# State attention of a fused transformer kernel: value products before state products, and both halves of four groups of work in a row between projections

## The chip, the cores and the metric

The kernel runs on one NeuronCore of a Trainium2 chip. A core has TensorE (PE in the profile; its weight loads are PEld), VectorE (DVE), ScalarE (ACT), GpSimd (POOL) and SyncE (SP), which issues the DMAs. Each engine works through its own list of instructions in order, and they meet at semaphores. The metric is the device time of one execution in microseconds; less is better.

## The reference

Four layers over 1024 tokens of 256 features, each an attention and a feed-forward part, run as one program. The change lies in the attention of layer 2, which goes through 64 slots per head:

```python
q = (hs @ Wq.T).reshape(B, T, H, DK)      # T = 1024 tokens in the kernel, H = 16, DK = DV = 128
k = (hs @ Wk.T).reshape(B, T, H, DK)      # both are rotated (rope)
v = (hs @ Wv.T).reshape(B, T, H, DV)
s = clip(hs @ Ws1.T @ Ws2.T + bs2)        # M = 64 slots per head
es = jnp.exp(s)
enz = jnp.exp(-cumlogsumexp(s))
A = where(mask, einsum('bhtd,bhjd->bhtj', q, k) * scale, 0.0)
ok = enz * jnp.einsum('bhtj,bhjm->bhtm', A, es)
qv = jax.nn.softmax(ok, axis=-1)
W2 = where(mask, einsum('bhtm,bhjm->bhtj', qv * enz, es), 0.0)
o = jnp.einsum('bhtj,bhjd->bhtd', W2, v)
o_n = o * rsqrt(mean(o * o) + EPS) * g_norm_weight
return (o_n * silu(g)).reshape(B, T, H * DV) @ Wo.T
```

## The kernel before

`state_attention` takes the 16 heads in eight pairs (`PAIRS`); the two heads of a pair are `a_` = 0 and 1. The 1024 tokens are eight blocks of 128 (`t`), four of them a half (`h` = 0 or 1, 512 tokens). The masked product over all earlier tokens is split: inside a block it is done with the 128x128 scores or weights (`atw`), and what lies before the block comes from a running state of 64 slots per head (`s1` for keys, `s2` for values), in which head 0 has partitions 0 to 63 and head 1 has 64 to 127.

One step `p` of the loop over pairs holds the work of pair `p`, the projections of pair `p + 1` and the last part of pair `p - 1`. TensorE's order is written out by hand in `_(pe)`, and so are those of ScalarE, VectorE and GpSimd. The groups of TensorE that matter here:

- `project(p + 1, c, h)` (q and k of the next pair): six fp32r matmuls of 128x512 (`gemm3`, line 718), and `out_product(p - 1, h, m)`, six alike.
- `turn_sums(p, h)` and `turn_soft(p, h)`: four transposes of 128x128 each (line 2437), of the sums over slots and of the softmax.
- `weights(p, h)`: W2 of a half, eight fp32 matmuls with 64 rows each, the two heads in the upper and the lower half of the array (`tile_position`, line 2532).
- `outputs(p, h)`: per block two value products with all 128 rows (`atw` by `v`, line 2549) and then two state products with 64 rows (`pb` by `s2`, line 2552), block by block; both add into the PSUM bank of the head. Block `t` = 0 has no state products.
- `key_states(p, h)` early in the step (line 2475): keys by exponentials of the slots.

Each PSUM bank (128x512) has a list of uses (`step_uses`), by which `opens` waits until the use before it has been emptied.

Who follows TensorE: `shift` (VectorE, maximum and difference behind `turn_sums`), `exp_soft` (ScalarE), `divide` (VectorE behind `turn_soft`), `copy_weights` (ScalarE, line 2664) and `mask_weights` (GpSimd, line 2853) behind `weights`; `outputs(p, h)` waits for the masks. Behind outputs come `square` (ScalarE, line 2748), `gate` (VectorE, line 3034) and `sum_squares` (3042). Behind each projection come `swap` (ScalarE, lines 2737 and 2738), `sines` (GpSimd, line 2873), `cosines` (VectorE, 3016) and `rotate` (VectorE, 3025). On VectorE the end of a step is gates of half 1, sums, rotations, and `clip` of the next pair's slot scores; then ScalarE takes their exponential (`exp_slots`, line 2672), then `root`, values and gates, and the key copies (`copy_keys`, line 2648) for which `key_states` waits.

Of the kernel before, what the change touches and what calls it, by code (L numbers as in the profile page):

```python
# [33 lines left out]
def half(h):  # L34
    return slice(h * HALF, (h + 1) * HALF)
# [2189 lines left out]
def state_attention(nc, core, a):  # L2225
# [18 lines left out]
        + [(("vg", 2, j), 0, 4 + j) for j in range(2)] + [(("ok", 0), 0, 0)]  # L2244
        + [(("to", 1, a_), -1, 2 + a_) for a_ in range(2)] + [(("ok", 1), 0, 1)]
        + [(("vg", 3, j), 0, 6 + j) for j in range(2)] + [(("s2", h), 0, 4 + h) for h in range(NH)]
# [3 lines left out]
        + [(("w2", 0, a_), 0, 2 + a_) for a_ in range(2)] + [(("q", 1, 1), 1, 7)]  # L2250
        + [(("w2", 1, a_), 0, a_) for a_ in range(2)] + [(("q", 2, 0), 1, 4)]
        + [(("o", 0, a_), 0, 2 + a_) for a_ in range(2)] + [(("q", 2, 1), 1, 5)]
        + [(("o", 1, a_), 0, a_) for a_ in range(2)] + [(("q", 3, 0), 1, 6), (("q", 3, 1), 1, 7)])
    uses = [(("ls", h), -1, h) for h in range(NH)]
    uses += [(k, s + dp, b) for s in range(-1, len(PAIRS)) for k, dp, b in step_uses if s + dp in PAIRS]
    uses += [(("to", 0, a_), LAST, 4 + a_) for a_ in range(2)] + [(("wo", 0, 0), LAST, 6), (("to", 1, 0), LAST, 2)]
# [15 lines left out]
    with ExitStack() as ctx:  # L2272
# [33 lines left out]
        v = sb("v", [P, TB, 2, DK])  # L2306
# [6 lines left out]
        atw = sb("atw", [P, TB, 2, P])  # L2313
# [18 lines left out]
        def bank(key):  # L2332
            return core.bank[bank_of[key]]
# [4 lines left out]
        def wait_emptied(eng, key):  # L2338
            b, n = emptying[key]
            eng.wait_ge(emptied[b], n)  # L2340
# [4 lines left out]
        def opens(pe, key):  # L2345
            if before[key] is not None:
                wait_emptied(pe, before[key])
# [41 lines left out]
        def _(pe):  # L2389
# [21 lines left out]
            def project(p, c, h):  # L2411
                if p not in PAIRS:
                    return
                key = ("q", p, c, h)
                pe.wait_ge(qkw_split, 2 * (4 * p + c) + 2)
                opens(pe, key)
                gemm3(pe, bank(key)[:, :], [qkwh[:, c, k * P:(k + 1) * P] for k in range(DC)],
                      [qkwl[:, c, k * P:(k + 1) * P] for k in range(DC)],
                      [core.xh[:, k, half(h)] for k in range(DC)],
                      [core.xl[:, k, half(h)] for k in range(DC)]).then_inc(full[bank_of[key]], 1)  # L2420
# [75 lines left out]
            def turn_sums(p, h):  # L2496
                if p not in PAIRS:
                    return
                wait_emptied(pe, ("ok", p, h))
                turn(("tok", p, h), lambda b: oke[:, (4 * h + b) * P:(4 * h + b + 1) * P])  # L2500
# [14 lines left out]
            def turn_soft(p, h):  # L2515
                if p not in PAIRS:
                    return
                pe.wait_ge(soft_exped, 2 * p + h + 1)
                turn(("tq", p, h), lambda b: qv[:, (4 * h + b) * P:(4 * h + b + 1) * P])
# [17 lines left out]
            def outputs(p, h):  # L2537
                if p not in PAIRS:
                    return
                keys = [("o", p, h, a_) for a_ in range(2)]  # L2540
                pe.wait_ge(w2_ready, 4 * p + 2 * h + 2)
                wait_emptied(pe, ("s2", p, h))
                opens(pe, keys[0])
                opens(pe, keys[1])
                for b in range(4):
                    t = 4 * h + b
                    for a_ in range(2):
                        out = bank(keys[a_])[:, b * P:(b + 1) * P]
                        mm = pe.matmul(out, atw[:, t, a_, :], v[:, t, a_, :], start=True, stop=t == 0)
                    for a_ in range(2 if t else 0):  # L2550
                        r = slice(64 * a_, 64 * a_ + 64)
                        mm = pe.matmul(bank(keys[a_])[:, b * P:(b + 1) * P], pb[r, t * P:(t + 1) * P], s2[r, t, :],
                                       start=False, stop=True, tile_position=(64 * a_, 0))
                        if b == 3:
                            mm.then_inc(full[bank_of[keys[a_]]], 1)

# [6 lines left out]
            def out_product(p, h, m):  # L2563
                if p not in PAIRS:
                    return
                key = ("wo", p, h, m)
                pe.wait_ge(wo_split, 2 * p + 2)
                wait_emptied(pe, ("to", p, h, 0))
                wait_emptied(pe, ("to", p, h, 1))
                opens(pe, key)  # L2570
                gemm3(pe, bank(key)[:, :], [woh[:, a_, m * P:(m + 1) * P] for a_ in range(2)],
                      [wol[:, a_, m * P:(m + 1) * P] for a_ in range(2)], [ogh[:, a_, half(h)] for a_ in range(2)],
                      [ogl[:, a_, half(h)] for a_ in range(2)]).then_inc(full[bank_of[key]], 1)
# [3 lines left out]
            for p in range(-1, len(PAIRS)):  # L2577
                turn_slots(p, 0)
                turn_slots(p, 1)
                turn_keys(p, 0, 0)  # L2580
                turn_keys(p, 0, 1)
                scores(p, 0, 0)
                scores(p, 0, 1)
                slot_scores(p + 1)
                values(p, 0)
                turn_keys(p, 1, 0)
                turn_keys(p, 1, 1)
                scores(p, 1, 0)
                scores(p, 1, 1)
                values(p, 1)  # L2590
                key_states(p, 0)
                key_states(p, 1)
                turn_out(p - 1, 0, 0)
                turn_out(p - 1, 0, 1)
                values(p, 2)
                slot_sums(p, 0)
                turn_out(p - 1, 1, 0)
                turn_out(p - 1, 1, 1)
                slot_sums(p, 1)
                values(p, 3)  # L2600
                value_states(p, 0)
                value_states(p, 1)
                out_product(p - 1, 0, 0)
                turn_sums(p, 0)
                out_product(p - 1, 0, 1)
                turn_sums(p, 1)
                out_product(p - 1, 1, 0)
                out_product(p - 1, 1, 1)
                project(p + 1, 0, 0)
                turn_soft(p, 0)  # L2610
                project(p + 1, 0, 1)
                turn_soft(p, 1)
                project(p + 1, 1, 0)
                weights(p, 0)
                project(p + 1, 1, 1)
                weights(p, 1)
                project(p + 1, 2, 0)
                outputs(p, 0)
                project(p + 1, 2, 1)
                outputs(p, 1)  # L2620
                project(p + 1, 3, 0)
                project(p + 1, 3, 1)
# [926 lines left out]
```

## Time and profile before

| | |
|---|---|
| median of 3 runs | 2773.91 us (2773.88 to 2775.19) |
| the profiled execution | 2764.51 us, its span 2762.8 us |
| TensorE busy | 2515.4 us, 91% of the span |
| VectorE, GpSimd, ScalarE busy | 1625.1, 1290.9, 1259.8 us |
| state attention | from about 1787 to 2286 us of the span |

How to read it: busy time is the sum of an engine's instructions. Records of TensorE's matmuls overlap (one of 0.40 us starts 0.23 us after the last), so in a list of its instructions the distance from start to start says what they cost. PEclk is the share of full clock granted to TensorE. In a timeline the columns are start, duration, engine, line, operation, what it writes and reads, count, and in brackets the idle time before it with what ended it.

### The profile page before, as it was taken

The page shows a single profiled execution, that of the slowest core. Times are in us where ns is not written, and L with a number is a line of the kernel's source. Part 1 is how long each engine was busy: PE and PEld are TensorE (multiplying, and loading weights), DVE is VectorE, ACT ScalarE, POOL GpSimd, SP SyncE. Part 2 cuts the span into 40 slices and gives each one's busy share as a digit, 9 for nine tenths or more (in the row PEclk, how much of TensorE's full clock was granted, in tenths as well). Part 3 has the DMA queues.
Part 4 walks back from the last instruction along what each step waited for, and adds up shares of the span by engine and source line. Part 5 has one row for each costly group of instructions (what it writes and reads, how often), then busy time and mean ns, then how long its engine had stood idle before and what let it go on. Part 6 is the DMA issues. An engine that isn't in the chain of part 4 may idle for free. (4 is left out here: it accounts for less than half of the span.)

```text
span 2762.8 us, 40694 instructions
## 1 busy us (share of the span) xinstructions
PE 2515.4 (91%) x14474; PEld 1675.7 (61%) x14474; DVE 1625.1 (59%) x2163; ACT 1259.8 (46%) x2174; POOL 1290.9 (47%) x1130
## 2 busy tenths in 40 slices
PE   6887999888999999999878878889999988998798
PEld 4443777654444444444564436678888877776676
DVE  4663555576766766665336543477777745555655
ACT  4464333464555555555434652256655643333322
POOL 4100344486888888888630002255454533442243
PEclk9798999998999999999976989899999999999899
DMA  1000111121101111010000001100010001110111
GB/s 59 1 2 11 39 46 46 48 80 39 39 16 39 31 31 39 16 35 1 25 26 1 1 1 49 47 20 28 20 32 20 20 5 42 46 46 21 31 41 43
DMA packets 39710, 81.63 MB, mean 30 GB/s; under 512 B 7553, under 2 KB 21121, under 8 KB 39041
## 3 DMA queue, kind: packets, MB, share of 16 engines
q1 hardware_dynamic: 39264, 79.41, 10.2%
q8 instruction: 98, 1.61, 0.2%
q14 instruction: 60, 0.48, 0.1%
q10 hardware_dynamic: 288, 0.13, 0.0%
HBM read 59.07 MB, written 2.62 MB: 22 GB/s over the span
## 5 line engine op out<-in xcount | busy, mean ns | idle before, releaser
L2019 DVE TENSOR_REDUCE a1h_mseg<-bank 128x2 f32<-128x1024 f32 x256 | 302.6, 1221 | 187.2 <-PE bank L1776 173.2
L63 POOL TENSOR_TENSOR f_wh<-f_raw,ones_r 128x768 fp32r<-128x768 f32 (+1 forms) x74 | 112.5, 1520 | 534.9 <-PE bank L462 360.0
L1953 ACT ACTIVATE a1h_prob<-bank 128x512 f32<-128x512 f32 x366 | 206.1, 598 | 165.6 <-PE bank L1836 83.8
L1756 POOL TENSOR_TENSOR a_qk<-a_qk,a1h_prob 128x512 f32<-128x512 f32 x186 | 238.9, 1318 | 50.8 <-ACT a1h_prob L1953 50.8
L451 PE MATMUL bank<-x_norm_h,f_wh 128*128 128x512 f32 x592 | 243.1, 411 | 6.7 <-PEq L3249 2.5
L451 PE MATMUL bank<-x_norm_l,f_wh 128*128 128x512 f32 x592 | 237.5, 401 | 0.0
L451 PE MATMUL bank<-x_norm_h,f_wl 128*128 128x512 f32 x592 | 237.0, 400 | 0.0
L658 DVE SCALAR_TENSOR_TENSOR f_tf<-bank,f_bias,f_sg 128x512 f32<-128x512 f32 x148 | 110.9, 750 | 187.2 <-PE bank L451 180.8
L542 ACT ACTIVATE f_hhi<-f_hf 128x512 fp32r<-128x512 f32 x124 | 78.3, 632 | 275.6 <-DVE f_hf L666 275.6
L1834 PE MATMUL bank<-a1h_ql,a1h_k 128*128 128x512 f32 x512 | 203.2, 397 | 0.0
L1849 PE MATMUL bank<-a1h_prob,a_v 128*64 128x512 f32 x732 | 179.9, 604 | 0.0
L672 DVE TENSOR_TENSOR f_hlo<-f_hf,f_hhi 128x512 fp32r<-128x512 f32 x124 | 116.2, 939 | 82.7 <-ACT f_hhi L542 82.4
L531 ACT ACTIVATE f_sg<-bank,f_bias 128x512 f32<-128x512 f32 x148 | 102.0, 689 | 128.4 <-PE bank L451 128.3
L451 PEld LDWEIGHTS bank<-x_norm_h,f_wh 128*128 128x128 f32 x592 | 113.5, 192 | 50.8 <-issue 24.3
L362 POOL TENSOR_TENSOR f_wl<-f_raw,f_wh 128x768 fp32r<-128x768 f32 (+1 forms) x74 | 128.0, 1730 | 5.9
L451 PEld LDWEIGHTS bank<-x_norm_l,f_wh 128*128 128x128 f32 x592 | 113.7, 192 | 28.1
L451 PEld LDWEIGHTS bank<-x_norm_h,f_wl 128*128 128x128 f32 x592 | 113.8, 192 | 24.9
L462 PE MATMUL bank<-f_hhi,f_wh 128*128 128x512 f32 x296 | 118.4, 400 | 10.4 <-DVE f_hlo L672 10.4
L1833 PE MATMUL bank<-x_norm_h,a1h_kn 128*128 128x512 f32 x256 | 120.4, 470 | 4.5 <-DVE a1h_k L2014 3.3
L2873 POOL TENSOR_TENSOR l2a_rope<-l2a_rope,l2a_tab 128x512 f32<-128x512 f32 x64 | 81.4, 1279 | 88.7 <-ACT l2a_rope L2738 87.7
L1756 POOL TENSOR_TENSOR x_norm<-x_norm,a1h_prob 128x512 f32<-128x512 f32 x86 | 112.4, 1340 | 20.5 <-ACT a1h_prob L1953 20.5
L1833 PE MATMUL bank<-x_norm_l,a1h_kn 128*128 128x512 f32 x256 | 118.6, 463 | 0.9
(597 smaller groups left out, 6277.1 us busy)
## 6 DMA issues: line engine op xcount, KB each, us to landing
f_raw<-in_l_w_dram SPq DMA_DIRECT2D x66, 385.0 KB, 3.0
a1h_st_q<-a_qk SPq DMA_DIRECT2D x128, 128.0 KB, 2.4
l2a_qkraw<-in_l2a_wqk_dram SPq DMA_DIRECT2D x32, 128.0 KB, 2.1
l2a_vraw<-in_l2a_wvg_dram SPq DMA_DIRECT2D x8, 512.0 KB, 3.7
f_raw<-in_l_w_dram SPq DMA_DIRECT2D x8, 449.0 KB, 3.3
a_qk<-l_keys SPq DMA_DIRECT2D x24, 128.0 KB, 2.7
a1p_raw<-in_l1a_w_dram SPq DMA_DIRECT2D x20, 128.0 KB, 2.1
a_qk<-in_l1a_wo_dram SPq DMA_DIRECT2D x16, 128.0 KB, 2.1
```

The source lines that it names most:

```text
L63: return pool.tensor_tensor(dst, src, one.to_broadcast(list(src.shape)), ALU.mult)
L362: pool.tensor_tensor(wl[:, slot, :], raw[:, slot, 0:B], wh[:, slot, :].bitcast(F32), ALU.subtract).then_inc(w_split, 1)
L451: mm = pe.matmul(out[:, :], w[:, slot, c0:c0 + P], x, start=n == 0, stop=n == 3 * n_k - 1)
L462: mm = pe.matmul(acc[m][h][:, :], w[:, slot, c0:c0 + P], x[:, h, :], start=begin and n == 0, stop=False, skip_group_check=True)
L658: dve.scalar_tensor_tensor(tf[:, h, :], up[h][:, :], bias[:, slot, 1:2], sg[:, h, :], ALU.add, ALU.mult).then_inc(t_ready, 1)
L672: dve.tensor_tensor(hl[:, h, :], src[:, h, :], hh[:, h, :].bitcast(F32), ALU.subtract).then_inc(hl_ready, 1)
L1756: pool.tensor_tensor(out, first, slot_of[t % NP], ALU.add).then_inc(sum_done, 1)
L1833: pe.matmul(bank[:, :], kn[:, G % 2, a, keys], QA[n % 2][:, a, half(h)], start=True, stop=False)
L1834: mm = pe.matmul(bank[:, :], k1[:, a, keys], ql[:, n % 2, a, half(h)], start=False, stop=lo >= hi)
L1849: pe.matmul(core.bank[5][64 * a:64 * a + 64, :], v[:, kb, 2 * (n // 4) + a, :], slot_of[t % NP], start=kb == 0, stop=kb == TB - 1, skip_gr ...
L1953: act.activation(slot_of[t % NP], core.bank[2 + t % 3][:, :], ACT.Exp, scale=scale).then_inc(p_ready, 1)
L2019: dve.tensor_reduce(mseg[:, :, qb, s], spare(("A", n, k))[:, :, :], AX.X, ALU.max).then_inc(a_read, 1)
```

## The change

Three things, all in `state_attention`. In `outputs` all value products of a half come first and its state products then, each half with one run of either (the `start` flag is now set for the first block of a bank alone). In TensorE's order both halves of `turn_sums`, of `turn_soft`, of `weights` and of `outputs` stand behind one another, between two projections or products, where a projection stood between the halves before. `step_uses` follows that order. The lists of the other engines are unchanged.

```diff
@@ step_uses
-        + [(("wo", 0, 0), -1, 0), (("tok", 0), 0, 2), (("wo", 0, 1), -1, 1), (("tok", 1), 0, 3)]
+        + [(("wo", 0, 0), -1, 0), (("wo", 0, 1), -1, 1), (("tok", 0), 0, 2), (("tok", 1), 0, 3)]
...
@@ outputs
                     for a_ in range(2):
                         out = bank(keys[a_])[:, b * P:(b + 1) * P]
-                        mm = pe.matmul(out, atw[:, t, a_, :], v[:, t, a_, :], start=True, stop=t == 0)
+                        mm = pe.matmul(out, atw[:, t, a_, :], v[:, t, a_, :], start=b == 0, stop=False,
+                                       skip_group_check=True)
+                for b in range(4):
+                    t = 4 * h + b
                     for a_ in range(2 if t else 0):
                         r = slice(64 * a_, 64 * a_ + 64)
                         mm = pe.matmul(bank(keys[a_])[:, b * P:(b + 1) * P], pb[r, t * P:(t + 1) * P], s2[r, t, :],
-                                       start=False, stop=True, tile_position=(64 * a_, 0))
+                                       start=False, stop=b == 3, tile_position=(64 * a_, 0), skip_group_check=True)
@@ the order of TensorE in a step
                 out_product(p - 1, 0, 0)
+                out_product(p - 1, 0, 1)
                 turn_sums(p, 0)
-                out_product(p - 1, 0, 1)
                 turn_sums(p, 1)
                 out_product(p - 1, 1, 0)
                 out_product(p - 1, 1, 1)
                 project(p + 1, 0, 0)
+                project(p + 1, 0, 1)
                 turn_soft(p, 0)
-                project(p + 1, 0, 1)
                 turn_soft(p, 1)
                 project(p + 1, 1, 0)
+                project(p + 1, 1, 1)
                 weights(p, 0)
-                project(p + 1, 1, 1)
                 weights(p, 1)
                 project(p + 1, 2, 0)
+                project(p + 1, 2, 1)
                 outputs(p, 0)
-                project(p + 1, 2, 1)
                 outputs(p, 1)
                 project(p + 1, 3, 0)
                 project(p + 1, 3, 1)
```

TensorE's list at the outputs of a pair before the change (value products are line 2549, state products 2552, a projection's matmuls line 718), from the first block on:

```order
L2549 MATMUL bank<-l2a_v,l2a_atw 128x128 x4
L2552 MATMUL bank<-l2a_s_,l2a_pb_ 128x128 x2
L2549 MATMUL bank<-l2a_v,l2a_atw 128x128 x2
L2552 MATMUL bank<-l2a_s_,l2a_pb_ 128x128 x2
L2549 MATMUL bank<-l2a_v,l2a_atw 128x128 x2
L2552 MATMUL bank<-l2a_s_,l2a_pb_ 128x128 x2
L718 MATMUL bank<-x_norm_h,l2a_qkwh 128x512
...
L2549 MATMUL bank<-l2a_v,l2a_atw 128x128 x2
L2552 MATMUL bank<-l2a_s_,l2a_pb_ 128x128 x2
```

The same place after the change (the lines have moved to 2550 and 2556):

```order
L718 MATMUL bank<-x_norm_l,l2a_qkwh 128x512
L2550 MATMUL bank<-l2a_v,l2a_atw 128x128 x8
L2556 MATMUL bank<-l2a_s_,l2a_pb_ 128x128 x6
L2550 MATMUL bank<-l2a_v,l2a_atw 128x128 x8
L2556 MATMUL bank<-l2a_s_,l2a_pb_ 128x128 x8
L718 MATMUL bank<-x_norm_h,l2a_qkwh 128x512
```

Seven runs of state products have become two, and the projection between the halves has moved ahead of both. At the weights (line 2532) TensorE's list before the change reads:

```order
L2532 MATMUL bank<-l2a_pb_,l2a_es_ 128x128 x8
L718 MATMUL bank<-x_norm_h,l2a_qkwh 128x512
L718 MATMUL bank<-x_norm_h,l2a_qkwl 128x512
L718 MATMUL bank<-x_norm_l,l2a_qkwh 128x512
L718 MATMUL bank<-x_norm_h,l2a_qkwh 128x512
L718 MATMUL bank<-x_norm_h,l2a_qkwl 128x512
L718 MATMUL bank<-x_norm_l,l2a_qkwh 128x512
L2532 MATMUL bank<-l2a_pb_,l2a_es_ 128x128 x8
```

And after the change (there it is line 2533), with the end of the projection that now stands ahead of them:

```order
L718 MATMUL bank<-x_norm_h,l2a_qkwh 128x512
L718 MATMUL bank<-x_norm_h,l2a_qkwl 128x512
L718 MATMUL bank<-x_norm_l,l2a_qkwh 128x512
L2533 MATMUL bank<-l2a_pb_,l2a_es_ 128x128 x16
L718 MATMUL bank<-x_norm_h,l2a_qkwh 128x512
```

Two runs of eight have become one of sixteen; the turns (line 2437) go from four and four to eight in the same way.

## Rows read from the trace of the kernel before

**Rows 1.** Stretches: busy us of PE, PEld, DVE, ACT, POOL, PEclk, DMA, GB/s; one step.

```profile
1957.00:2015.50 58.50, 58.03 (x422) 48.04 (x418) 42.10 (x64) 34.53 (x57) 29.06 (x31) 1.00 0.08 23
```

**Rows 2.** Timeline of TensorE, weights and outputs of one step.

```profile
1968.81 1.16 PE L2532 MATMUL bank<-l2a_pb_,l2a_es_ 64*128 64x128 f32 x16
1969.90 0.51 PE L718 MATMUL bank<-x_norm_h,l2a_qkwh 128*128 128x512 f32 x1
...
1973.87 0.39 PE L718 MATMUL bank<-x_norm_l,l2a_qkwh 128*128 128x512 f32 x1
1974.10 1.05 PE L2549 MATMUL bank<-l2a_v,l2a_atw 128*128 128x128 f32 x8
1975.08 0.49 PE L2552 MATMUL bank<-l2a_s_,l2a_pb_ 64*128 64x128 f32 x4
1975.50 0.71 PE L2549 MATMUL bank<-l2a_v,l2a_atw 128*128 128x128 f32 x4
1976.14 0.49 PE L2552 MATMUL bank<-l2a_s_,l2a_pb_ 64*128 64x128 f32 x4
...
1977.63 0.50 PE L718 MATMUL bank<-x_norm_h,l2a_qkwh 128*128 128x512 f32 x1
...
1979.13 0.61 PE L2549 MATMUL bank<-l2a_v,l2a_atw 128*128 128x128 f32 x4
1979.67 0.49 PE L2552 MATMUL bank<-l2a_s_,l2a_pb_ 64*128 64x128 f32 x4
...
1983.28 0.51 PE L718 MATMUL bank<-x_norm_h,l2a_qkwh 128*128 128x512 f32 x1
```

**Rows 3.** Timeline of TensorE, turns of four and of eight.

```profile
1966.89 0.60 PE L2437 MATMUL bank<-ident,x_norm 128*128 128x128 f32 x4
1967.24 0.48 PE L718 MATMUL bank<-x_norm_h,l2a_qkwh 128*128 128x512 f32 x1
1967.56 0.40 PE L718 MATMUL bank<-x_norm_h,l2a_qkwl 128*128 128x512 f32 x1
...
1986.18 1.03 PE L2437 MATMUL bank<-ident,l2a_es_ 128*128 128x128 f32 x8
```

**Rows 4.** Timeline of TensorE, before the key states of the next pair.

```profile
1998.73 0.40 PE L718 MATMUL bank<-l2a_vgl,x_norm_h 128*128 128x512 f32 x1
1999.34 3.31 PE L2475 MATMUL bank<-l2a_estm,l2a_ktm 128*128 128x64 f32 x28 [0.21 <-ACT l2a_ktm L2648]
```

**Rows 5.** Timeline of VectorE, gates of half 0 to gates of half 1.

```profile
1978.36 1.29 DVE L3034 TENSOR_TENSOR l2a_og<-bank,l2a_g 128x512 f32<-128x512 f32 x2 [1.72 <-ACT l2a_sq L2748]
...
1981.35 0.68 DVE L3025 TENSOR_TENSOR l2a_qt<-bank,l2a_rope 128x512 f32<-128x512 f32 x1
1984.01 1.29 DVE L3034 TENSOR_TENSOR l2a_og<-bank,l2a_g 128x512 f32<-128x512 f32 x2 [1.98 <-ACT l2a_sq L2748]
```

**Rows 6.** Timeline of ScalarE, copies of the weights, then exponential and key copies.

```profile
1970.01 1.09 ACT L2664 ACTIVATE l2a_atw<-bank 128x512 f32<-128x512 f32 x2 [1.71 <-PE bank L2532]
...
1973.59 1.09 ACT L2664 ACTIVATE l2a_atw<-bank 128x512 f32<-128x512 f32 x2
...
1992.08 1.06 ACT L2672 ACTIVATE l2a_es_<-l2a_es_ 128x1024 f32<-128x1024 f32 x1 [1.06 <-DVE l2a_es_ L2939]
...
1998.49 1.08 ACT L2648 ACTIVATE l2a_ktm<-bank 128x512 f32<-128x512 f32 x2
```

**Rows 7.** Timeline of GpSimd, sines of two projections and masks of half 1.

```profile
1972.41 2.54 POOL L2873 TENSOR_TENSOR l2a_rope<-l2a_rope,l2a_tab 128x512 f32<-128x512 f32 x2 [0.51 <-ACT l2a_rope L2738]
1974.89 1.23 POOL L2853 TENSOR_SCALAR_AFFINE_SELECT l2a_atw<-l2a_atw 128x512 f32<-128x512 f32 x2
```

**Rows 8.** Timeline of VectorE in the last step, shift of half 1 and divisions.

```profile
2252.85 0.69 DVE L2989 TENSOR_REDUCE l2a_mx<-bank 128x8 f32<-128x512 f32 x1 [0.41 <-PE bank L2437]
...
2257.76 1.28 DVE L3007 TENSOR_TENSOR l2a_pb_<-bank,l2a_enz_ 128x512 f32<-128x512 f32 x2
```

More of the change, by code:

```diff
@@ L2246, in state_attention @@
         + [(("vg", 3, j), 0, 6 + j) for j in range(2)] + [(("s2", h), 0, 4 + h) for h in range(NH)]
[1 row of a table removed]
[1 row of a table added]
         + [(("wo", 1, 0), -1, 6), (("wo", 1, 1), -1, 7)]
[1 row of a table removed]
[L2250 to L2253, printed above, removed]
[2 rows of a table added]
+        + [(("w2", 0, a_), 0, 2 + a_) for a_ in range(2)] + [(("w2", 1, a_), 0, a_) for a_ in range(2)]
+        + [(("q", 2, 0), 1, 4), (("q", 2, 1), 1, 5)]
+        + [(("o", 0, a_), 0, 2 + a_) for a_ in range(2)] + [(("o", 1, a_), 0, a_) for a_ in range(2)]
+        + [(("q", 3, 0), 1, 6), (("q", 3, 1), 1, 7)])
     uses = [(("ls", h), -1, h) for h in range(NH)]
```

3 rows, old and new, of the table step_uses are left out of this document.

## Prediction

> **What bounds the kernel now.** I read the table of stretches first, because the change lives in one stage. Over one step of the state attention TensorE is busy 58.03 of 58.5 us at a granted clock of 1.00, VectorE 42.1, ScalarE 34.5 and GpSimd 29.1 [rows 1]. So the stage is as long as TensorE's own list; the other engines matter only where they make it wait. Next I read TensorE's timeline through weights and outputs [rows 2], looking not at durations but at the distance from one start to the next, since matmuls overlap. The reader is to see that the same number of records takes very different times there. Then the turns [rows 3], the one place where TensorE waits each step [rows 4], and the queues of VectorE [rows 5], ScalarE [rows 6] and GpSimd [rows 7] behind it, because the change shortens the cover that hides them.
>
> **What a switch costs.** An fp32 matmul leaves two records. Value products use all 128 rows of the array; state products and weights use two tiles of 64 rows, and two of their records run side by side. In the outputs of half 0 a block of four state records takes 1975.08 to 1975.50 = 0.42 us and the block of four value records behind it 1975.50 to 1976.14 = 0.64 [rows 2], together 1.06. Without a switch: eight value records take 0.98 up to the next start and four take 0.54 (1979.13 to 1979.67), so one is (0.98 - 0.54) / 4 = 0.11 and four are 0.44; sixteen weights records take 1968.81 to 1969.90 = 1.09, so a pair is (1.09 - 0.42) / 6 = 0.11 and two pairs are 0.22 [rows 2]. That is 0.66, and an excursion into half rows and back costs 1.06 - 0.66 = 0.40 us. The value products' entry behind a projection costs nothing (1973.87 to 1974.10 = 0.23, the step of a projection's own matmuls). That the state products add onto what the value products wrote is not what is paid: the way back to value products, which reads nothing of the state products' columns, is as dear. The Trainium skill, "TensorEngine Tiling (Array Packing)", section Key Properties, says that changing the tiling mode, and not just the tile, drains TensorE; by that rule the price goes with the number of changes, and the trace agrees with about 0.2 us at each edge.
>
> **The change, part by part.** (a) Outputs: half 0 makes three excursions now and half 1 four; afterwards one each. Five go: 5 x 0.40 = 2.0 us a step. The flags start and skip_group_check add no instruction: nothing. (b) Weights of both halves stand together: two excursions become one, 0.40. I take the same price as in outputs; the bounds are nothing and 0.40, and six of the eight steps pay it alike. (c) Turns of sums and of softmax in pairs. A single turn of four is 1966.89 to 1967.24 = 0.35, and the matmul behind it 1967.24 to 1967.56 = 0.32 instead of 0.23; eight in a row last 1.03 against 0.60 for four [rows 3], that is 0.43 more. Two singles: 2 x (0.35 + 0.09) = 0.88; one run of eight: 0.35 + 0.43 + 0.09 = 0.87. Worth nothing. (d) DMAs, and the lists of ScalarE, VectorE, GpSimd and SyncE, are unchanged. So TensorE's list gets 2.4 us shorter in each of the first seven steps; in the last, where no projections of a next pair exist and weights and outputs stand together already, only outputs gain: 2.0.
>
> **What comes late.** Half 0 of each group now starts one projection later (1.4 us), half 1 where it was. I follow each queue behind them.
> Masks. From the start W of the weights of half 0: copies at +1.20 (1970.01), the copies of half 1 at +4.78 (1973.59) [rows 6], sines at +3.60, masks of half 1 at +6.08 and done 1.23 later, at W + 7.31 [rows 7]. These queues run without a hole and are the same after the change. TensorE reaches the outputs of half 1 at W + 1.99 (both weights: 1.09 + 8 x 0.11) + 0.10 + 2 x 1.41 (two projections, the first behind a switch) + outputs of half 0 (1974.10 to 1977.63 = 3.53 before, less two excursions = 2.73), so at W + 7.6. Before it was 1979.13 - 1968.81 = 10.3. The cover shrinks from 3.0 to 0.3 us: still enough, narrowly.
> Gates. VectorE starts gating half 0 0.73 after the end of its outputs (1977.63 to 1978.36), needs 2.99 up to the rotation at 1981.35 and 0.60 for it [rows 5], so half 1 can't be gated before 0.73 + 3.59 = 4.32. Outputs of half 1 lasted 1979.13 to 1983.28 = 4.15 [rows 2]; less three excursions, and with the 0.10 that their first matmul pays behind half 0's state products, they will last 3.05 and would be ready for VectorE at 3.05 + 0.73 = 3.78. VectorE comes 0.54 us late. Before, it had waited 1.98 there [rows 5]. From there it has no hole up to the clipping of the next pair's scores, for which ScalarE waits (1.06 before its exponential at 1992.08), and ScalarE has none from there to the key copies at 1998.49 [rows 6], for which TensorE waits: 1998.73 to 1999.34 is 0.61 instead of 0.23 [rows 4]. This wait has no slack left, so all 0.54 is added: 0.38 becomes 0.92. It is there in steps 1 to 6 (the last has no exponential in the chain): 6 x 0.54 = 3.2 us given back. Its bounds are nothing (if VectorE's queue has a hole that I don't see) and the same 0.54 in all seven, 3.8.
> The Trainium skill says in "TensorEngine Tiling (Array Packing)", section PSUM Bottleneck, that after tiling has sped TensorE up the copies out of PSUM may become the bottleneck. That rule speaks against the change; it gives no figure, and the row shows VectorE's emptying late by 0.54 of 2.4 us.
> The softmax of half 1 is shifted 0.95 later on VectorE (both halves' sums now arrive together, two passes of 0.7 for each), which projections cover in steps 0 to 6. In the last step nothing covers it, since VectorE works without a hole from the shift to the divisions [rows 8]: 0.95 lost. The outputs' gain there, 2.0 for half 1 and 0.80 for half 0, arrives through the chain of gates, square root and scaling; I take the middle, 1.4. Net 0.4 (bounds -0.2 and 1.0).
>
> **Sum.** 7 x 2.4 = 16.8, less 3.2, plus 0.4: 14.0 us. The profiled execution took 2764.5 (span 2762.8 and 1.7 around it) and becomes 2750.5; the median of the runs is 2773.9, 0.34% above it, and 14 us are the same there within 0.05: 2760. About 0.2%, 5.5 us, is what a measurement of this kernel can tell from no change.
>
> **Rivals.**
> 1. The cover holds everywhere: gates are not late and the wait at the key states stays 0.38. For it: VectorE is busy only 42.1 of 58.5 [rows 1]. Against: its queue is dense exactly there [rows 5]. 16.8 + 0.4 gives 2756.7. Chance 0.15.
> 2. The masks of half 1 come late, by one sine product more than I count (1.3 us). For: 0.3 us of slack. Against: the queue is read off the trace without a gap. A wait before the outputs of half 1 first eats the slack of 0.3 and then the 0.54 that VectorE would have been late anyway, so it costs (1.3 - 0.3 - 0.5) x 7 = 3.5: 2763.5. Chance 0.12.
> 3. The 0.40 in outputs is paid for something else than the switch, such as adding onto a bank just written, and stays. Then only the weights gain, 7 x 0.40 = 2.8: 2771, no measurable change. Against: both edges cost alike. Chance 0.06.
> 4. Slower: TensorE's clock. The granted clock is 1.00 through the stage [rows 1], and stretches at 0.5 stand in the profile where TensorE has holes. If the new 0.9 us wait, or the denser outputs, brought stretches at half clock, each microsecond of them would give back half a microsecond. It decides from 28 us on (the whole gain), and 40 us make the kernel slower by 6: 2780. Against: a wait of 0.38 and the short ones of the start of the step left the clock at 1.00. Chance 0.04.
> The forecast has 0.60; 0.03 is left for what I don't name, a third of it each way.
>
> **How the numbers follow.** Faster: 0.60 + 0.15 + 0.12 + 0.01 = 0.88. Same: 0.06 + 0.01, rounded up to 0.08. Slower: 0.04, with the rest of the unnamed in it. The forecast's own bounds: the weights' excursion at nothing takes 2.8 (2762.8); no backlog gives 2756.7; the last step 0.6 either way; two bounds at once, weights at nothing and masks late, 2766. A sum over 7 x 6 + 5 = 47 excursions at 0.02 of rounding each adds 1. The range 2754 to 2766 holds the forecast, rivals 1 and 2.
>
> **What the profile of the changed kernel would show.** Outputs of half 0 in two blocks, 16 value and 12 state records, 2.7 us, and of half 1 3.05; weights one block of 32 records, 2.0 us; turns in eights with no gain. A step of 58.5 - 2.4 + 0.54 = 56.7 us. TensorE's distance before the key states 1.15 instead of 0.61, and VectorE without a wait before the gates of half 1. No wait on the masks before the outputs of half 1, or one under 0.2. Granted clock 1.00. I would be wrong if a block of 16 state records took more than 1.1 us, if the outputs of half 1 began with a wait of over 0.9 us on GpSimd, or if the turns moved the softmax so that the weights wait.

## The result, and the profile after

The changed kernel took 2761.85 us (median of 11 runs, 2756.26 to 2767.13) and the kernel before 2773.91 (median of 11 runs made beside them, 2766.10 to 2779.05). The ratio is 0.9961 with a 95% interval of 0.9948 to 0.9973: 10.8 us less by the ratio, 7.5 to 14.4 (the two medians lie 12.1 apart). The forecast was 2760 and 14.0 us less.

The profiled execution took 2761.3 us, against 2764.5 before: only 3 us less, although the stage itself became 14 us shorter. The table of stretches shows why. These are the stretches before the stage, its steps up to the softmax turns of the last step, the last part (from those turns to the next norm), and everything behind it; columns as in [rows 1]. First the kernel before:

```profile
0.00:1768.83 1768.83, 1589.80 (x9223) 933.96 (x9223) 1003.46 (x1189) 829.48 (x1485) 883.82 (x738) 0.92 0.11 28
1768.83:2220.38 451.55, 431.86 (x2996) 354.26 (x2997) 318.47 (x467) 254.59 (x413) 219.75 (x231) 0.97 0.09 28
2220.38:2287.01 66.63, 55.62 (x410) 46.16 (x408) 31.34 (x61) 28.95 (x50) 17.91 (x21) 0.97 0.01 2
2287.01:2762.80 475.79, 438.15 (x1848) 341.34 (x1848) 271.83 (x447) 146.80 (x229) 169.46 (x141) 0.94 0.13 39
```

and the changed kernel, with one step (the first line) that answers to [rows 1]:

```profile
1930.00:1986.19 56.19, 55.68 (x420) 47.38 (x419) 41.29 (x64) 34.56 (x57) 29.10 (x32) 1.00 0.08 24
...
0.00:1775.62 1775.62, 1597.70 (x9223) 936.92 (x9223) 1001.42 (x1189) 829.49 (x1485) 884.28 (x738) 0.92 0.11 28
1775.62:2210.45 434.83, 415.48 (x2996) 349.43 (x2997) 313.15 (x466) 254.57 (x413) 219.57 (x231) 0.97 0.09 29
2210.45:2279.69 69.24, 57.47 (x410) 48.39 (x408) 31.38 (x62) 28.80 (x50) 18.08 (x22) 0.90 0.02 5
2279.69:2759.60 479.91, 442.49 (x1848) 345.76 (x1848) 272.12 (x447) 146.74 (x229) 169.28 (x141) 0.93 0.13 39
```

The reader is to see three things. The steps gave 451.55 - 434.83 = 16.7 us. The last part lost 2.6, at a granted clock of 0.90 instead of 0.97. And the code before and behind the stage, which is the same in both kernels, was longer by 6.8 and 4.1 in this execution. TensorE's clock has two levels, 2.4 GHz (1.00) and 1.2 (0.50); counted record by record, the first stretch had 17 us more at the lower level and the last one 10.5. Between all executions profiled here the stretch ahead of the stage took 1768 to 1782 us and the one behind it 476 to 483, moving with that count. So one execution's total can't tell 5 us; what can is the length of a step, which has a clock of 1.00 throughout and repeats within 0.15 us.

TensorE's timeline of the changed kernel, weights to the softmax turns of one step, answers to [rows 2] and [rows 3]:

```profile
1912.11 1.03 PE L2438 MATMUL bank<-ident,x_norm 128*128 128x128 f32 x8
1912.90 0.48 PE L718 MATMUL bank<-x_norm_h,l2a_qkwh 128*128 128x512 f32 x1
...
1915.87 2.06 PE L2533 MATMUL bank<-l2a_pb_,l2a_es_ 64*128 64x128 f32 x32
1917.86 0.51 PE L718 MATMUL bank<-x_norm_h,l2a_qkwh 128*128 128x512 f32 x1
...
1920.76 1.95 PE L2550 MATMUL bank<-l2a_v,l2a_atw 128*128 128x128 f32 x16
1922.64 0.94 PE L2556 MATMUL bank<-l2a_s_,l2a_pb_ 64*128 64x128 f32 x12
1923.51 2.05 PE L2550 MATMUL bank<-l2a_v,l2a_atw 128*128 128x128 f32 x16
1925.49 1.16 PE L2556 MATMUL bank<-l2a_s_,l2a_pb_ 64*128 64x128 f32 x16
1926.58 0.50 PE L718 MATMUL bank<-x_norm_h,l2a_qkwh 128*128 128x512 f32 x1
```

Weights of both halves are 1.99 us from start to start. Outputs of half 0 are 1920.76 to 1923.51 = 2.75 (forecast 2.7), of half 1 1923.51 to 1926.58 = 3.07 (3.05). No line has a bracket, so TensorE waits for nothing here.

The one wait of each step, which answers to [rows 4] (the first line is the last matmul of the value projection, the second the key states):

```profile
1942.04 0.40 PE L718 MATMUL bank<-l2a_vgl,x_norm_h 128*128 128x512 f32 x1
1942.68 3.31 PE L2476 MATMUL bank<-l2a_estm,l2a_ktm 128*128 128x64 f32 x28 [0.25 <-ACT l2a_ktm L2652]
```

The distance is 0.64 us. It was 0.61 before and 1.15 in the forecast: this is where the forecast is wrong. VectorE's timeline in the changed kernel, from gates of half 0 to the clipping of the next pair's scores, answers to [rows 5]:

```profile
1924.24 1.29 DVE L3038 TENSOR_TENSOR l2a_og<-bank,l2a_g 128x512 f32<-128x512 f32 x2 [0.55 <-ACT l2a_sq L2752]
...
1927.82 1.28 DVE L3038 TENSOR_TENSOR l2a_og<-bank,l2a_g 128x512 f32<-128x512 f32 x2
...
1930.20 0.72 DVE L3053 TENSOR_TENSOR l2a_rs<-l2a_rs 128x16 f32<-128x16 f32 x1
1930.96 0.17 DVE L3056 SCALAR_TENSOR_TENSOR l2a_norm_f<-l2a_rs,l2a_ss 128x16 f32<-128x16 f32 x1
...
1934.04 1.28 DVE L2943 TENSOR_SCALAR l2a_es_<-bank 128x512 f32<-128x512 f32 x2
```

Gates of half 1 have lost their wait, as forecast, and stand 1.67 us ahead of the softmax turns (1929.49) where they stood 1986.18 - 1984.01 = 2.17 ahead [rows 3, 5]: 0.50 late. But from there to the clipping VectorE needed 1934.04 - 1927.82 = 6.22 us, and before it 6.69, as these lines of the kernel before show:

```profile
1986.40 1.18 DVE L3049 TENSOR_TENSOR l2a_rs<-l2a_rs 128x16 f32<-128x16 f32 x1
1987.62 0.18 DVE L3052 SCALAR_TENSOR_TENSOR l2a_norm_f<-l2a_rs,l2a_ss 128x16 f32<-128x16 f32 x1
...
1990.70 1.28 DVE L2939 TENSOR_SCALAR l2a_es_<-bank 128x512 f32<-128x512 f32 x2
```

0.46 of the 0.47 us is one tiny instruction, the square of the state sums (128x16): it lasted 1.18 before and 0.72 after, where a similar one beside it needs 0.17. GpSimd's timeline, of the kernel before and of the changed one, holds the reason:

```profile
1986.28 1.28 POOL L2873 TENSOR_TENSOR l2a_rope<-l2a_rope,l2a_tab 128x512 f32<-128x512 f32 x1 [2.03 <-ACT l2a_rope L2738]
```

```profile
1929.62 1.28 POOL L2877 TENSOR_TENSOR l2a_rope<-l2a_rope,l2a_tab 128x512 f32<-128x512 f32 x1
```

Before, the sine product ends at 1987.56 and VectorE's square at 1987.58; after, at 1930.90 and 1930.92. It is so in all seven steps of both traces: the square, issued earlier or later, ends 0.03 to 0.04 behind the sine product (by the unrounded records). It holds a wait inside its duration.

### The profile page after: what moved, and what is told of

It reads as the page before. It is cut to its first block and busy times, and to the rows that moved or that the text cites. A ratio compares the mean times of both kernels' runs of the same rounds, so it can differ in the third digit from the quotient of the medians.

```text
span 2759.6 us, 40694 instructions
## 1 busy us (share of the span) xinstructions
PE 2513.1 (91%) x14474; PEld 1680.5 (61%) x14474; DVE 1618.1 (59%) x2163; ACT 1259.6 (46%) x2174; POOL 1291.2 (47%) x1130
## 5 line engine op out<-in xcount | busy, mean ns | idle before, releaser
L462 PE MATMUL bank<-f_hhi,f_wh 128*128 128x512 f32 x296 | 118.4, 400 | 10.8 <-DVE f_hlo L672 10.8
L1457 ACT ACTIVATE a2h_prob<-bank 128x512 f32<-128x512 f32 (+3 forms) x192 | 83.7, 488 | 81.3 <-PE bank L1287 56.8
```

The costliest lines, as they stand in the source:

```text
L462: mm = pe.matmul(acc[m][h][:, :], w[:, slot, c0:c0 + P], x[:, h, :], start=begin and n == 0, stop=False, skip_group_check=True)
```

## The experiments

A step is the median distance between the starts of the turns of es (the exponentials of the slots, line 2437 or 2438, once a step), steps 1 to 6; "distance" is from TensorE's last value-projection matmul to the key states; "last" is from the turns of es in the last step to the next norm, with the us of it at half clock; "stage" runs from the norm ahead of it to the norm behind it. Where an edit changes TensorE's order, `step_uses` follows it; that part is not printed below.

```
kernel                    step    distance   last (half clock)   stage
before                    58.52   0.60       66.63  (3.4)        518.2
changed                   56.19   0.64       69.24 (13.7)        504.1
e1_blocks_only            56.56   0.60       66.02  (6.8)        504.0
e2_order_only             58.12   0.60       68.77  (6.8)        517.2
e3_early_square           56.11   0.56       66.83  (6.8)        501.1
e4_turns_apart            56.21   0.63       65.81  (6.8)        501.3
e8_mean_late              56.10   0.56       66.80  (6.8)        501.0
e10_before_both_moved     58.49   0.56       66.66  (3.4)        518.3
e11_slot_sums             57.17   0.63       67.02 (10.2)        507.5
e9_all                    57.12   0.56       66.41 (10.2)        506.8
e12_keys_first            55.69   0.23       69.18 (13.7)        500.8
e13_row_keys_first        55.02   0.23       65.60  (6.8)        493.5
```

**Outputs regrouped, nothing else.** The kernel before, with the outputs' loop of the changed one:

```diff
                     for b in range(4):
                         t = 4 * h + b
-                        mm = pe.matmul(out, atw[:, t, a_, :], v[:, t, a_, :], start=True, stop=t == 0)
+                        mm = pe.matmul(out, atw[:, t, a_, :], v[:, t, a_, :], start=b == 0, stop=False,
+                                       skip_group_check=True)
+                for b in range(4):
+                    t = 4 * h + b
...
-                                       start=False, stop=True, tile_position=(64 * a_, 0))
+                                       start=False, stop=b == 3, tile_position=(64 * a_, 0), skip_group_check=True)
```

> The order of before, with the value products of a half ahead of its state products and nothing else. The price of a switch between full and half rows (0.39 us for an excursion and back) is my theory: 3 + 4 excursions become 1 + 1, five go, so a step of steps 1 to 6 takes 58.52 - 5 x 0.39 = 56.55 us. The distance before the key states stays 0.60. Rival: the blocks gain only next to each other (it is the neighbourhood of both halves that pays), then a step stays near 58.5 less at most 0.4.

Measured: step 56.56, so 1.96 us less than before, 5 x 0.39; one run of 2756.80 beside 2769.98 of the kernel before. TensorE's timeline:

```profile
1972.64 1.95 PE L2549 MATMUL bank<-l2a_v,l2a_atw 128*128 128x128 f32 x16
1974.52 0.94 PE L2555 MATMUL bank<-l2a_s_,l2a_pb_ 64*128 64x128 f32 x12
1975.39 0.50 PE L718 MATMUL bank<-x_norm_h,l2a_qkwh 128*128 128x512 f32 x1
...
1982.77 1.03 PE L2437 MATMUL bank<-ident,l2a_es_ 128*128 128x128 f32 x8
```

The outputs of half 0 are 2.75 long in the old order too. The regrouping alone is worth 1.96 of the step's 2.33.

**The order, nothing else.** The changed kernel with the outputs block by block:

```diff
-                        mm = pe.matmul(out, atw[:, t, a_, :], v[:, t, a_, :], start=b == 0, stop=False,
-                                       skip_group_check=True)
-                for b in range(4):
-                    t = 4 * h + b
+                        mm = pe.matmul(out, atw[:, t, a_, :], v[:, t, a_, :], start=True, stop=t == 0)
...
```

> The order of after, with the value and state products block by block as before. By the price of a switch only the weights' excursion goes: five excursions more than after, a step of 56.19 + 5 x 0.39 = 58.15 us. Rival: neighbourhood pays, then a step near 56.2 to 57.

Measured: step 58.12, 0.40 less than before; one run of 2767.32 beside 2769.98. That is one excursion, the weights'. 1.96 + 0.40 = 2.36, and the changed kernel has 2.33, with a distance before the key states that is 0.04 longer: the two parts add up. Its last part took 68.77, 2.14 more than before with 3.4 us more at half clock.

**The square of the state sums at once.** If VectorE's backlog sets the key states' wait, taking the hidden wait away should shorten it:

```diff
+            def square_sums(p):
+                if p not in PAIRS or p == LAST:
+                    return
...
                 dve.tensor_tensor(rs[:, :, :], rs[:, :, :], rs[:, :, :], ALU.mult).then_inc(mean_sq, 1)
+
+            def mean_squares(p):
...
                 sum_rows(p, 1)
+                square_sums(p)
```

> After, with one small instruction of VectorE (the square of the softmax's row sums, 128x16, both operands and the result in SBUF) moved from behind the gates of half 1 to right behind the row sums. It lasts 1.18 us before and 0.72 after, ends in both within 0.03 us of the end of GpSimd's sine product that runs beside it, and takes 0.16 in the last step, where GpSimd is idle. Theory: it waits for GpSimd to end, and this hidden wait had swallowed the lateness of the gates that I had forecast. Moved to where GpSimd is idle it takes 0.16 to 0.2; VectorE's chain to the clipping gets 0.55 shorter, the distance before the key states falls from 0.64 to 0.23, and a step takes 56.19 - 0.41 = 55.78 us. Rival: the instruction is long for itself and the gates were never late; then it lasts 0.7 to 1.2 in its new place too and the step stays 56.2.

Measured: step 56.11, distance 0.56; one run of 2755.28 beside 2769.98. VectorE's timeline shows the square at 0.17 us where it now stands, and the next instruction with two inputs in SBUF, which had needed 0.17 before, in its place and with its wait:

```profile
1965.89 0.17 DVE L3053 TENSOR_TENSOR l2a_rs<-l2a_rs 128x16 f32<-128x16 f32 x1
...
1984.83 0.53 DVE L3060 SCALAR_TENSOR_TENSOR l2a_norm_f<-l2a_rs,l2a_ss 128x16 f32<-128x16 f32 x1
```

GpSimd's timeline of the same place:

```profile
1984.05 1.27 POOL L2877 TENSOR_TENSOR l2a_rope<-l2a_rope,l2a_tab 128x512 f32<-128x512 f32 x1
```

It ends at 1985.32, and VectorE's instruction at 1985.36. So the wait hangs on the sine product, whichever instruction meets it; whether VectorE's lateness matters was still open.

**Both instructions out of the way.** The same, and the mean of squares behind the last rotation; and the same two moves on the kernel before:

```diff
-                else:
-                    mean_squares(p)
                 rotate(p + 1, 2, 1)
...
                 rotate(p + 1, 3, 1)
+                if p < LAST:
+                    mean_squares(p)
```

> e3 and the second of the two small VectorE instructions that read SBUF twice (row sums by sums of squares, 128x16) moved too, behind the last rotation, where GpSimd has finished its last sine product. In e3 it had taken over the wait: 0.53 us instead of 0.17, with its end again at the end of GpSimd's sine product. Theory (VectorE waits for GpSimd's instruction to end): now nothing of VectorE that reads SBUF twice stands beside a sine product, the instruction takes 0.17, the distance before the key states falls from 0.56 to 0.23 to 0.25, and a step takes 56.11 - 0.33 = 55.8 us. Rival: the chain is pinned elsewhere (rotations that need the sines), then the step stays 56.1.

> The kernel before, with the same two small VectorE instructions moved as in e8. If VectorE's wait for GpSimd (1.0 us here) is what makes the key states wait, the distance before them falls from 0.60 to 0.23 and a step from 58.52 to 58.15 us. In this kernel the gates of half 1 are not late, so this tells the hidden wait apart from the gates. Rival: no change, 58.5.

Measured: 56.10 and 58.49, and a distance of 0.56 in both; one run each, 2765.30 and 2780.02, both with a longer stretch ahead of the stage. No wait of the old kind is left, and the steps are only 0.09 and 0.03 shorter than those of the kernels they started from, where 0.4 was expected. VectorE's timeline of the first says where the rest of the time went:

```profile
1994.29 0.16 DVE L3060 SCALAR_TENSOR_TENSOR l2a_norm_f<-l2a_rs,l2a_ss 128x16 f32<-128x16 f32 x1
1995.06 1.29 DVE L2943 TENSOR_SCALAR l2a_es_<-bank 128x512 f32<-128x512 f32 x2 [0.61 <-PE bank L2409]
```

and TensorE's:

```profile
1990.58 1.03 PE L2438 MATMUL bank<-ident,l2a_es_ 128*128 128x128 f32 x8
...
1994.54 0.71 PE L2409 MATMUL bank<-l2a_low,l2a_slots_w 128*128 128x512 f32 x2
```

VectorE is early by 0.61 us and waits for TensorE's own slot scores (L2409), which come 3.96 us behind the turns. The clipping starts 4.48 behind them (1995.06 - 1990.58), in the changed kernel 4.55, before 4.52. My theory that VectorE's queue sets the key states' wait is refuted: that queue is at best 0.07 us from the floor. What is left between the clipping and the key states is ScalarE.

**Key copies ahead of values and gates, on ScalarE.** The changed kernel; TensorE needs the keys of head 1 before the first values:

```diff
                 root(p - 1)
-                copy_values(p, 0)
-                gates(p, 0)
                 copy_keys(p, 1, 0)
                 copy_keys(p, 1, 1)
                 copy_scores(p, 1, 0)
                 copy_scores(p, 1, 1)
+                copy_values(p, 0)
+                gates(p, 0)
                 copy_values(p, 1)
```

> After, with ScalarE's copies of the keys and scores of head 1 moved ahead of its copies of the first values and their gates (with its table load). e8 and e10 showed VectorE idle before the clipping, so the chain to the key states now starts at TensorE's slot scores and runs through clipping, exponential, square root with two table loads, values and gates on ScalarE. If ScalarE's queue behind the exponential is what the key states wait for, the copies come 2.4 us earlier, the distance before the key states falls from 0.64 to 0.23 and a step from 56.19 to 55.8 us. Rival: the distance is made by something else, or the values that come later make TensorE wait elsewhere; then 56.2.

Measured: step 55.69, distance 0.23; one run of 2762.61 beside a median of 2776.19 of the kernel before. ScalarE's timeline in the changed kernel:

```profile
1935.42 1.06 ACT L2676 ACTIVATE l2a_es_<-l2a_es_ 128x1024 f32<-128x1024 f32 x1 [1.09 <-DVE l2a_es_ L2943]
...
1939.44 0.58 ACT L2700 ACTIVATE l2a_v<-bank 128x512 f32<-128x512 f32 x1
1940.04 1.28 ACT L2707 ACT_TABLE_LOAD   x1
1941.34 0.60 ACT L2707 ACTIVATE l2a_g<-bank 128x512 f32<-128x512 f32 x1
1941.83 1.08 ACT L2652 ACTIVATE l2a_ktm<-bank 128x512 f32<-128x512 f32 x2
```

and in this one:

```profile
1993.26 1.06 ACT L2676 ACTIVATE l2a_es_<-l2a_es_ 128x1024 f32<-128x1024 f32 x1 [1.10 <-DVE l2a_es_ L2943]
...
1997.28 1.07 ACT L2652 ACTIVATE l2a_ktm<-bank 128x512 f32<-128x512 f32 x2
```

From exponential to key copies it is 6.41 us in the first and 4.02 in the second. The values' copy, a table load of 1.28 for the gates and the gate itself had stood in front. The exponential still waits 1.10 us for VectorE, and TensorE no longer waits at all: the whole wait was ScalarE's order. The step gained 0.50, 0.41 of it in that distance.

**Turns apart again.** The changed kernel with the turns of sums and softmax interleaved as before:

```diff
                 out_product(p - 1, 0, 0)
-                out_product(p - 1, 0, 1)
                 turn_sums(p, 0)
+                out_product(p - 1, 0, 1)
...
                 project(p + 1, 0, 0)
-                project(p + 1, 0, 1)
                 turn_soft(p, 0)
+                project(p + 1, 0, 1)
```

> After, with the turns of the sums and of the softmax apart again, one projection or product between the halves as before. The row says that pairs of turns gain nothing, so steps 1 to 6 stay at 56.19 us. In step 0, which has no output products as cover, TensorE's wait for the softmax may grow by up to 0.5. In the last step the weights start 0.9 us earlier after the key states (25.8 instead of 26.7 us), since half 0 is not held back. Rival: the pairs of turns save a switch each, then steps 1 to 6 grow by 0.2 to 0.8.

Measured: step 56.21, so pairing the turns is worth nothing (0.02) in steps 1 to 6. In step 0 it is worth 0.38: that step took 52.33 here and 51.95 in the changed kernel, whose turns waited 0.7 us for ScalarE's softmax where these waited 1.3. The last part took 65.81, and 66.83 in e3_early_square, which has the turns in pairs and as much half clock: 1.0 less. TensorE's timeline, key states and weights of the last step:

```profile
2216.87 3.23 PE L2476 MATMUL bank<-l2a_estm,l2a_ktm 128*128 128x64 f32 x28
...
2242.69 2.06 PE L2533 MATMUL bank<-l2a_pb_,l2a_es_ 64*128 64x128 f32 x32 [2.04 <-DVE l2a_pb_ L3011]
```

The weights start 25.82 behind the key states, and in the changed kernel 26.71. One run of 2754.88, 6.97 under the changed kernel's median; the stage is 2.8 shorter, and the rest lies in code that is the same in both.

**Two excursions more.** If each is worth 0.40 wherever it stands, the slot sums of both heads, side by side and next to the value states, should give two:

```diff
                 values(p, 2)
-                slot_sums(p, 0)
                 turn_out(p - 1, 1, 0)
                 turn_out(p - 1, 1, 1)
-                slot_sums(p, 1)
                 values(p, 3)
+                slot_sums(p, 0)
+                slot_sums(p, 1)
                 value_states(p, 0)
```

> After, with two more excursions of TensorE taken out: the values of blocks 6 and 7 and the turns of half 1 of the last pair's output now come ahead of both halves of the slot sums, which then stand in a row with the value states (all three use tiles of 64 columns). By 0.39 us for an excursion a step takes 56.19 - 0.8 = 55.4 us, if no wait takes its place. Rival: the slot sums of half 0 come 4 us later, and VectorE's chain from them to the turns of the sums makes TensorE wait; then 56.2 or more.

> All that helped: after, with both small instructions moved (e8), the slot sums in a row (e11), and the turns apart as in e4. Steps of 56.19 - 0.4 - 0.8 = 55.0 us, 3.5 us a step less than before the change, and over the whole about 26 us less than before: a ratio of 0.990 to 0.992. If the waits of e8 and e11 are the same wait, 55.4.

The second is this with turns apart and both moves on VectorE. Measured: steps of 57.17 and 57.12, longer than the changed kernel's 56.19. e9_all took 2759.49 (median of 12 runs) against 2771.64 of the kernel before (17 runs), ratio 0.9948, 0.9928 to 0.9968: not to be told from the changed kernel's 0.9961, where 0.990 to 0.992 was expected. Both are misses, and TensorE's timeline of e11_slot_sums names the cause:

```profile
2013.93 0.40 PE L718 MATMUL bank<-l2a_vgl,x_norm_h 128*128 128x512 f32 x1
2015.59 1.28 PE L2438 MATMUL bank<-ident,l2a_og 128*128 128x128 f32 x8 [1.26 <-DVE l2a_ogl L3078]
2016.63 0.48 PE L718 MATMUL bank<-l2a_vgh,x_norm_h 128*128 128x512 f32 x1
```

I had moved the turns of half 1 of the last pair's output forward past the slot sums, and they now need a bank that VectorE's L3078 frees later. From start to start the matmul ahead of the turns takes 1.66 us instead of 0.23, and the turns 1.04 instead of the 0.80 of turns without a wait: 1.67 a step. With two excursions less by the 0.67 measured below, that makes 56.19 - 0.67 + 1.67 = 57.19, and the step has 57.17. The list of waits has it six times, 7.6 us in total:

```profile
PE bank L2438 <- DVE l2a_ogl L3078: 7.6, 6, 1.3
```

**The same behind all values, with keys first and turns apart.** The edits of e12_keys_first and e4_turns_apart, and this one on the changed kernel:

```diff
                 values(p, 2)
-                slot_sums(p, 0)
+                values(p, 3)
                 turn_out(p - 1, 1, 0)
                 turn_out(p - 1, 1, 1)
+                slot_sums(p, 0)
                 slot_sums(p, 1)
-                values(p, 3)
```

> e12, the turns apart as in e4, and the slot sums in a row with the value states, but with the turns of half 1 of the last pair's output behind the values of blocks 6 and 7, where VectorE has freed their banks (in e11 they waited 1.4 us for it). Two excursions of 0.39 us less: steps of 55.8 - 0.8 = 55.0 us, and over the whole 7 x 3.5 = 25 us less than before the change, a ratio of 0.991. Rival: the sums of half 0 come late for VectorE and a wait takes the place of the excursions, then 55.8 or more and a ratio near 0.993.

Measured: step 55.02, stage 493.5, and 2747.74 us (median of 6 runs) against 2776.19 (11 runs), ratio 0.9895, 0.9872 to 0.9918: 29 us less than before (23 to 36), the best of the kernels here. TensorE's timeline, turns of half 1 of the output:

```profile
2000.38 1.03 PE L2438 MATMUL bank<-ident,l2a_og 128*128 128x128 f32 x8
```

The turns have no bracket: one projection later VectorE is done. The two excursions here are worth 55.69 - 55.02 = 0.67, 0.33 each; these are products in tiles of 64 columns, not of 64 rows.

## Why the prediction was right, and where it was not

Time and direction were right, and the stage of the profiled execution went from 518.2 to 504.1, 14.1 less. But that sum is right by luck: two errors of 3.2 and 3.0 us cancel.

**The price of an excursion, 0.40: right.** e1_blocks_only gives 5 x 0.39 for the outputs and e2_order_only 0.40 for the weights, apart and additive. Rival 3, that the price is paid for adding onto a bank, is refuted: the additions are all still there.

**Turns in pairs, nothing: right** in steps 1 to 6 (e4_turns_apart: 0.02).

**Masks late (rival 2): refuted, as forecast.** Outputs of half 1 begin at 1923.51 without a wait. GpSimd's masks, of the changed kernel, end at 1923.16, 0.35 ahead (forecast 0.3):

```profile
1921.94 1.22 POOL L2857 TENSOR_SCALAR_AFFINE_SELECT l2a_atw<-l2a_atw 128x512 f32<-128x512 f32 x2
```

**The gates' backlog: wrong, and this is the step that failed.** "This wait has no slack left, so all 0.54 is added" was to give back 6 x 0.54 = 3.2 us. The gates were late by 0.50, but the distance at the key states grew by 0.03 to 0.04: 0.2 us in six steps. VectorE's queue had slack that looked like work: "From there it has no hole up to the clipping" held by the timeline, but one 128x16 instruction lasted 1.18 us instead of 0.17, waiting for GpSimd's sine product, and took up what came late. I should have asked why 16 elements cost 1.18 us. The bound "nothing (if VectorE's queue has a hole that I don't see)" and rival 1 had the outcome, at a chance of 0.15: the wait at the key states stayed. Rival 1's reason, that the gates are not late, was not the true one. The step came out at 56.19, where the forecast had 56.7 and rival 1 58.5 - 2.4 = 56.1.

What sets that wait instead is ScalarE's order (e12_keys_first). e8_mean_late and e10_before_both_moved show that without any hidden wait VectorE's clipping moves only up to TensorE's own slot scores, 0.04 to 0.07 earlier behind the turns than in the two kernels of the change.

**The first steps: 7 x 2.4 = 16.8 forecast before anything given back, and 16.8 measured** between the softmax turns of the first and of the last step (405.9 before, 389.1 after). Steps 1 to 6 gave 14.1 together (2.33 in the median) and step 0 2.75. What step 0 gave beyond 2.4 lies in its turns in pairs, by 0.38 (e4_turns_apart); the forecast had them at nothing there.

**The last step: +0.4 forecast, -2.6 measured.** Its two terms can be read between kernels with the same 6.8 us at half clock. The later softmax costs 1.0 (e4_turns_apart against e3_early_square; forecast 0.95), and the regrouped outputs give 68.77 - 66.83 = 1.94 (e2_order_only against e3_early_square; forecast 1.4). e1_blocks_only, which has e4_turns_apart's order in this part, took 0.2 more than it, so these are good to about 0.2. At an equal clock the last part would then have gained 0.9, not 0.4. The rest is TensorE's clock, which the forecast had left at 1.00. In the changed kernel TensorE ran 13.7 us of this part at 1.2 GHz, and e3_early_square and e8_mean_late, with the same order in it, 6.8: they take 66.8 instead of 69.24. TensorE's timeline shows the place, from the start of the outputs of half 0 to the start of those of half 1, in the changed kernel:

```profile
2252.60 3.79 PE L2550 MATMUL bank<-l2a_v,l2a_atw 128*128 128x128 f32 x16 [0.66 <-POOL l2a_atw L2857]
...
2257.86 2.05 PE L2550 MATMUL bank<-l2a_v,l2a_atw 128*128 128x128 f32 x16
```

and in e3_early_square:

```profile
2250.52 2.05 PE L2550 MATMUL bank<-l2a_v,l2a_atw 128*128 128x128 f32 x16 [1.08 <-POOL l2a_atw L2857]
...
2253.37 2.05 PE L2550 MATMUL bank<-l2a_v,l2a_atw 128*128 128x128 f32 x16
```

Both start 42.15 us behind the softmax turns (2210.45 and 2208.37). From there half 0 takes 5.26 us at the lower level and 2.85 at the upper: 2.41 more, which is the whole difference of the two last parts. That is 2.4 for 6.8 us, 0.35 for each. By that price, an estimate for the 3.4 us that also separate the changed kernel from the one before, 13.7 instead of 3.4 us are 3.6, and 0.9 - 3.6 = -2.7 against a measured -2.6. That e12_keys_first, at 13.7 us again, took 69.18 fits. Where the stretch falls matters: e9_all, with 10.2 us, took 66.41 and e13_row_keys_first, with 6.8, 65.60, so 0.24 for each there. In kind this is rival 4, in the last part only; in the steps the clock stayed at 1.00. Whether the change makes the larger count more likely, or whether it falls by chance as in the identical stretches around the stage, is open: the kernels with its order in the last part had 6.8, 6.8, 13.7 and 13.7 us (and e2_order_only 6.8), the kernel before and e10_before_both_moved 3.4 twice.

**The sum.** 16.8 from the steps, 0.9 and -3.6 from the last part make 14.1, and the stage of that execution measured 14.1. The forecast reached 14.0 with 3.2 too much taken off in the steps and 3.0 too little in the last part. Of the whole kernel the ratio gives 10.8 and the medians 12.1; the interval up to 14.4 holds both 14.0 and 14.1. What separates these lies within what the identical code around the stage varies by.

## What to carry to other kernels

Group matmuls by how they tile the array before asking anything else of their order: each excursion into tiles of half the rows or half the columns and back cost 0.33 to 0.40 us here, with no wait to be seen in any bracket, and splitting one loop in two gave five sixths of the gain. Before counting a queue as full, compare each instruction's duration with its size: one of 128x16 that lasts 1.18 us is a wait, and is slack for what comes late ahead of it. And when a wait names an engine, walk its queue back from the instruction named and ask what stands in front without need; here a copy, a table load and a gate, 2.4 us, could go behind.

## What the runs showed of the hardware

A VectorE instruction with two inputs in SBUF waits for a GpSimd instruction that is under way, and the wait is part of its recorded duration: 0.16 to 0.18 us alone, 0.53 to 1.19 beside the sine product (128x512, 1.28). In the three places shown, and in all seven steps of each of the nine kernels here that have such an instruction in that place, it ends 0.03 to 0.04 behind the sine product by the unrounded records; moved away from it, in e3_early_square, e8_mean_late and e10_before_both_moved, it is short. VectorE's reductions (one input, in SBUF; two of them in 1.27 us) and rotations (one input in PSUM and one in SBUF; 0.68) kept these durations in the same places. The Trainium skill, "SBUF — State Buffer", section "SBUF: two separate sides", calls the port pair that VectorE and GpSimd share "an exclusive lock, not a bandwidth split", taken also by a VectorE operation with two SBUF inputs against a GpSimd operation that reads SBUF. The trace agrees with it: the ends at 1987.56 and 1987.58, and at 1930.90 and 1930.92.

Identical code took 1768 to 1782 us in one stretch and 476 to 483 in another from execution to execution, with 266 to 311 and 58 to 75 us of them at half clock. Of a kernel of 2.77 ms that is more than this change was worth; the length of a step at full clock repeated within 0.15 us.
